# Unpacking 4-bit weights beside a matmul stream: integer codes on VectorE replaced by float arithmetic spread over VectorE and ScalarE

## The reference

```
xn = layernorm(x)
x  = x + gated_cumsum_attention(xn) + moe(xn)      # block 0: shared expert and 8 routed, top 2
xn = layernorm(x)
x  = x + latent_attention(xn) + ffn(xn)            # block 1
```

```
LUT = [0, .5, 1, 1.5, 2, 3, 4, 6, -0, -.5, -1, -1.5, -2, -3, -4, -6]
idx = stack([W & 15, W >> 4 & 15], -1)              # two codes a word
W_f32 = LUT[idx] * scale of its block of 32
```

## Time and profile before

| | us |
|---|---|
| median of 3 runs | 919.44 |
| lowest and highest | 918.81, 920.84 |
| the profiled execution | 919.44 |
| its span in the trace | 917.1 |
| TensorE matmul busy in the span | 796.1 (87%) |
| VectorE, ACT, GpSimd busy | 524.1 (57%), 435.9 (48%), 347.7 (38%) |

### The profile page before, as it was taken

How to read it: one execution, slowest core, us unless ns; L and a number is a source line. 1 busy time by engine, 2 the same in 40 slices (tenths; PEclk the granted TensorE clock), 3 DMA queues, 4 the chain that set the end, 5 groups by cost and what they waited for, 6 DMA issues and landing times.

```text
span 917.1 us, 12644 instructions
## 1 busy us (share of the span) xinstructions
PE 796.1 (87%) x4756; PEld 600.8 (66%) x4756; DVE 524.1 (57%) x871; ACT 435.9 (48%) x675; POOL 347.7 (38%) x277
## 2 busy tenths in 40 slices
PE   3759989998998899988898899798898897998886
PEld 1537866776676677766666677576676675776664
DVE  4742666675667633645464746564755656664735
ACT  3442433442434243352735754827645648536454
POOL 2333334662455242441342432424332515133533
PEclk9899999997999999998999999999999999999999
DMA  6331033332233125471110030110130200120100
GB/s 210 108 108 47 12 92 92 103 104 93 78 92 98 66 92 202 158 277 47 31 42 1 1 97 21 41 30 1 32 84 1 71 1 1 40 53 22 50 2 24
DMA packets 62171, 62.48 MB, mean 68 GB/s; under 512 B 6176, under 2 KB 52128, under 8 KB 61344
## 3 DMA queue, kind: packets, MB, share of 16 engines
q1 hardware_dynamic: 59680, 58.37, 20.6%
q10 hardware_dynamic: 2432, 3.32, 1.1%
HBM read 32.18 MB, written 16.78 MB: 53 GB/s over the span
## 4 chain that ended last, share of the span: by engine, by line
PE 53%; ACT 15%; DVE 13%; issue 10%; POOL 4%; DMA 4%; SPq 1%; ACTq 0%; DVEq 0%; POOLq 0%
PE ring L418 6%; PE ring L420 6%; PE ring L419 6%; PE acc L418 4%; PE acc L419 4%; PE acc L420 4%; ACT act L1027 3%; ACT L1027 2%; ACT ex L1027 2%; PE pm L418 2%; POOL hl L1128 2%; DVE hf L1392 2%; PE pm L420 2%; PE pm L419 2%; DMA x1s<-x 2%
## 5 line engine op out<-in xcount | busy, mean ns | idle before, releaser
L1128 POOL TENSOR_TENSOR hl<-hf,hh 128x512 fp32r<-128x512 f32 (+1 forms) x120 | 159.2, 1326 | 428.5 <-ACT hh L906 427.1
L418 PE MATMUL ring<-xh,wh 128*128 128x512 f32 (+1 forms) x272 | 114.0, 419 | 18.5 <-DVE xl L1226 13.4
L906 ACT ACTIVATE hh<-hf 128x512 fp32r<-128x512 f32 (+1 forms) x120 | 75.3, 627 | 92.1 <-DVE hf L1392 86.2
L418 PE MATMUL acc<-hh,wh 128*128 128x512 f32 (+1 forms) x240 | 101.2, 422 | 16.1 <-POOL hl L1128 16.1
L419 PE MATMUL ring<-xh,wl 128*128 128x512 f32 (+1 forms) x272 | 108.8, 400 | 0.0
L420 PE MATMUL ring<-xl,wh 128*128 128x512 f32 (+1 forms) x272 | 108.7, 400 | 0.0
L419 PE MATMUL acc<-hh,wl 128*128 128x512 f32 (+1 forms) x240 | 97.1, 405 | 0.0
L420 PE MATMUL acc<-hl,wh 128*128 128x512 f32 (+1 forms) x240 | 96.9, 404 | 0.0
L1286 DVE TENSOR_TENSOR hf<-act,ring 128x512 f32<-128x512 f32 (+1 forms) x56 | 38.3, 683 | 89.6 <-ACT act L896 86.6
L660 PE MATMUL ring<-qT,kT 98*128 98x256 bf16 (+1 forms) x256 | 45.6, 249 | 39.5 <-ACT ex L1027 20.3
L418 PEld LDWEIGHTS ring<-xh,wh 128*128 128x128 f32 (+1 forms) x272 | 52.0, 191 | 39.7 <-DVE xl L1226 16.3
(11 more groups left out here) (194 smaller groups left out, 1931.7 us busy)
## 6 DMA issues: line engine op xcount, KB each, us to landing
w4s<-w4h SPq DMA_DIRECT2D x24, 256.0 KB, 2.3
w4s<-w4l SPq DMA_DIRECT2D x24, 256.0 KB, 3.0
qT<-qp SPq DMA_DIRECT2D x96, 64.0 KB, 2.6
kT<-kp SPq DMA_DIRECT2D x96, 64.0 KB, 2.7
stage<-w SPq DMA_DIRECT2D x6, 704.0 KB, 5.5
wh<-w4s SPq DMA_DIRECT2D x2, 2048.0 KB, 9.4
wl<-w4s SPq DMA_DIRECT2D x2, 2048.0 KB, 14.3
words<-q SPq DMA_DIRECT2D x12, 256.0 KB, 3.3
```

Of the source, the lines that this page charges most:

```text
L418: pe.matmul(o, w_hi, x_hi, start=first, stop=False, skip_group_check=True)
L906: a.activation(h_parts(n)[0][0:rows, :], hf[0:rows, n % 2, :], ACT.Copy).then_inc(s_hh, 1)
L1128: return pool.tensor_tensor(dst, src, hi.bitcast(F32), ALU.subtract)
```

## The change

The float value of a code is now made by arithmetic. For each step VectorE shifts the three magnitude bits m to bit 22 of a 32-bit word and ORs a constant into the exponent (`fbits`), and puts the sign bit into `sbits`. ACT computes `gval = 8 * fbits - 1`. VectorE then takes `min(4 * fbits, gval)`, which is the value of the table, and ORs the sign in. GpSimd multiplies by the scale, which is used as it is, and has one buffer in place of two.

In VectorE's order the last two (value and sign of code k-1) stand at the beginning of step k, ahead of the three bit instructions for code k. ACT's `gval` of step k stands behind `w4h` in its step k and waits for the bits of step k.

```diff
-        mag = sb("mag", [P, QW], U16, c0)
-        sign = sb("sign", [P, QW], U16, c0)
-        code = sb("code", [P, 2, QW], U16, c0)
-        scl = sb("scl", [P, 2, QW], F32, c0)
+        fbits = sb("fbits", [P, QW], I32, c0)
+        sbits = sb("sbits", [P, QW], I32, c0)
+        gval = sb("gval", [P, 2, QW], F32, c0)
+        scl = sb("scl", [P, QW], F32, c0)
...
# SyncE
-                            sp.wait_ge(s_bits, 4 * (n - 1))
+                            sp.wait_ge(s_bits, 6 * (n - 1))
...
-                if k % 2 == 0:
-                    for n in (0, 1) if k == 0 else (k // 2 + 1,) if k // 2 + 1 < NQ else ():
-                        if n >= 2:
-                            sp.wait_ge(s_w, k)
-                        sp.dma_start(scl[:, n % 2, :], s4[:, n, :]).then_inc(s_scl[n % 2], 16)
+                if k % 2 == 0 and k < 2 * NQ:
+                    if k:
+                        sp.wait_ge(s_w, k)
+                    sp.dma_start(scl[:, :], s4[:, k // 2, :]).then_inc(s_scl, 16)
...
# ACT, behind w4h
-                if 0 <= k < 2 * NQ and k % 2 == 0:
-                    n = k // 2
-                    a.wait_ge(s_scl[n % 2], 16 * (n // 2 + 1))
-                    a.activation(scl[:, n % 2, :], scl[:, n % 2, :], ACT.Copy, scale=F4_UNIT).then_inc(s_sfit, 1)
+                if 0 <= k < 2 * NQ:
+                    a.wait_ge(s_bits, 3 * (k + 1))
+                    a.activation(gval[:, k % 2, :], fbits[:, :].bitcast(F32), ACT.Copy, bias=-1.0,
+                                 scale=8.0).then_inc(s_val, 1)
...
# GpSimd, behind w4l
-                    pool.wait_ge(s_code, k)
-                    pool.wait_ge(s_sfit, (k - 1) // 2 + 1)
+                    pool.wait_ge(s_sgn, 2 * k)
+                    pool.wait_ge(s_scl, 16 * ((k - 1) // 2 + 1))
...
-                    pool.tensor_tensor(wf[:, :], code[:, (k - 1) % 2, :].bitcast(F16), scl[:, (k - 1) // 2 % 2, :],
-                                       ALU.mult).then_inc(s_w, 1)
+                    pool.tensor_tensor(wf[:, :], gval[:, (k - 1) % 2, :], scl[:, :], ALU.mult).then_inc(s_w, 1)
...
# VectorE, dequant(k)
+                if 1 <= k < 2 * NQ + 1:
+                    v.wait_ge(s_val, k)
+                    val = gval[:, (k - 1) % 2, :]
+                    v.scalar_tensor_tensor(out=val, in0=fbits[:, :].bitcast(F32), scalar=4.0, in1=val, op0=ALU.mult,
+                                           op1=ALU.min).then_inc(s_sgn, 1)
+                    v.wait_ge(s_sgn, 2 * k - 1)
+                    v.tensor_tensor(val.bitcast(u32), val.bitcast(u32), sbits[:, :].bitcast(u32),
+                                    ALU.bitwise_or).then_inc(s_sgn, 1)
...
                     if k:
-                        v.wait_ge(s_code, k)
-                    low16 = words[:, k // 2 % 2, :].bitcast(U16).rearrange("p (n h) -> p n h", h=2)[:, :, 0]
-                    v.tensor_scalar(mag[:, :], low16, 9 - 4 * j, 7 << 9, ALU.logical_shift_left,
+                        v.wait_ge(s_sgn, 2 * k)
+                    w32, f32 = words[:, k // 2 % 2, :].bitcast(u32), fbits[:, :].bitcast(u32)
+                    v.tensor_scalar(f32, w32, 22 - 4 * j, 7 << 22, ALU.logical_shift_left,
                                     ALU.bitwise_and).then_inc(s_bits, 1)
-                    v.tensor_scalar(sign[:, :], low16, 12 - 4 * j, 1 << 15, ALU.logical_shift_left,
+                    v.tensor_scalar(sbits[:, :].bitcast(u32), w32, 28 - 4 * j, 1 << 31, ALU.logical_shift_left,
                                     ALU.bitwise_and).then_inc(s_bits, 1)
-                    v.wait_ge(s_bits, 2 * k + 2)
-                    if k >= 2:
-                        v.wait_ge(s_w, k - 1)
-                    v.tensor_tensor(code[:, j, :], mag[:, :], sign[:, :], ALU.bitwise_or).then_inc(s_code, 1)
+                    v.wait_ge(s_bits, 3 * k + 2)
+                    v.tensor_scalar(f32, f32, 124 << 23, None, ALU.bitwise_or).then_inc(s_bits, 1)
```

More of the change, by code:

```diff
@@ L77 @@
 Q0 = 8
-F4_UNIT = 2.0 ** 14
 W4_CUTS = [0, 4096, O_D4, O_D4 + 6 * D, O_D4 + T1 * D]
@@ L235, in transformer_blocks @@
         s_words = [sem(f'words_in{i}') for i in range(2)]
-        s_scl = [sem(f"scales_in{i}") for i in range(2)]
-        s_bits, s_sfit, s_code, s_w, s_w4h, s_w4l = map(
-            sem, ("bit_steps", "scales_fitted", "codes", "w4", "w4_hi", "w4_split"))
+        s_scl, s_bits, s_val, s_sgn, s_w, s_w4h, s_w4l = map(
+            sem, ("scales_in", "bit_steps", "values", "signs", "w4", "w4_hi", "w4_split"))
         s_w4out, s_w4in = [sem(f"w4_stored{i}") for i in range(2)], [sem(f"w4_in{i}") for i in range(4)]
@@ L1263, in turn_weights @@
                 v.tensor_tensor(own, own, part(0), ALU.add).then_inc(s_turnw, 1)
+            u32 = mybir.dt.uint32
             def dequant(k):
+                if 1 <= k < 2 * NQ + 1:
[6 more added lines that the diff above has]
+                                    ALU.bitwise_or).then_inc(s_sgn, 1)
                 if 0 <= k < 2 * NQ:
```

## The result

The changed kernel takes 961.23 us (median of four runs, 960.31 to 962.33); the kernel before takes 919.17 on the same chip (918.81 to 920.84). The ratio is 1.046, 95% interval 1.0445 to 1.0477: 42 us slower. The forecast was 955, with 930 to 976 as its range. The profiled execution took 962.32 us, its span 959.9 against 917.1 before.

The account below looks back on a forecast made before the run. TensorE was taken to set the pace, 4.43 us a tile, with VectorE and GpSimd excluding each other. Group growths of 5, 16, 12 and 2 us sum to +35, plus 1 for the clock: 919.4 + 36 = 955, range 930 to 976.

Parts of the forecast that it names:

- The odd tile: Second tile of each pair with unpacking steps: `act` to next `act` 7.45 us instead of 5.83.
- D1: VectorE's `scalar_tensor_tensor` making the value (4x against ACT's value), two float32 inputs: 0.69 us alone.
- D2: VectorE's OR of the sign into the value, two float32 inputs: 0.69 us alone.
- The crammed free and even tile: Tile without a step, then the next pair's first tile: together 9.1 us, a three-tile cycle of 16.55 against 13.3.
- fifth rival: Cycle right but pace milder, as GpSimd and VectorE do not meet everywhere: about 935; chance 0.12.
- The lock: Two-input VectorE instructions and GpSimd's exclude each other; without this the sum is near +15 us, with it +36.
- D3 to D5: VectorE's two shifts and OR on 32-bit words that make the bits: 0.42 us each alone, other end 0.69.
- third rival: The three 32-bit bit instructions take 0.69 us each: +19 less overlap, 971; chance 0.10.
- ACT's wait: `gval` waits for VectorE in 24 steps, 40 us or more; the `wf` wait shrinks below 58.5 or moves into it.
- The group ends: Time not given back where a group ends with a step: 3.35 us in the second group, 1.5 in the third.
- The four growths: Growth of the first block's four token groups: +5, +16, +12 and +2 us.
- fourth rival: Single scale buffer: scales land late for the odd step, 1 us in each of 12 places at worst; 960; chance 0.05.

Follow-up runs that it names:

- load_alone: Kernel before, with two more two-input float32 VectorE instructions at the head of each step, on spare data: 933.24 us, ratio 1.0134.
- change_ends: Changed kernel with the last tile's step put behind the next group's `xh` on ACT and `xl` on VectorE: 950.46 us, ratio 1.0331.
- before_w4h_late: Kernel before, with ACT's `w4h` alone one tile later, except in a group's last tile: 914.12 us, ratio 0.994.
- before_late_ends: before_w4h_late with the last tile's step behind the next group's `xh` on ACT and `xl` on VectorE: 908.06 us, ratio 0.9867.
- act_late_ends: act_late with the last tile's step behind the next group's `xh` on ACT and `xl` on VectorE: 920.47 us, ratio 1.0001.
- act_late: bits_first with ACT's `w4h` and `gval` one tile later, except in a group's last tile: 930.83 us, ratio 1.0107.
- bits_first: Changed kernel with float16 `gval`, 16-bit sign, and VectorE's bit instructions of code k ahead of value and sign of code k-1: 931.39 us, ratio 1.0132.

## Why the prediction was right

**The odd tile.** Predicted 7.45 us, measured 7.51. From `act` = 0, predicted and measured ends: D1 3.0 and 3.02, `w4l` 4.2 and 4.17, D2 4.75 and 4.72, `wf` 5.9 and 5.86, D5 6.9 and 6.94. The odd tiles of the second and third group that have no table load take 7.47 to 7.61.

**The crammed free and even tile.** Predicted 9.1, measured 9.27 (ACT's timeline of the changed kernel, third group):

```profile
272.73 0.58 ACT L893 ACTIVATE act<-ring 128x512 f32<-128x512 f32 x1
273.73 0.58 ACT L893 ACTIVATE act<-ring 128x512 f32<-128x512 f32 x1
...
281.46 0.63 ACT L886 ACTIVATE gval<-fbits 128x512 f32<-128x512 f32 x1 [2.94 <-DVE fbits L1285]
282.00 0.58 ACT L893 ACTIVATE act<-ring 128x512 f32<-128x512 f32 x1
```

A cycle of three tiles is 16.8 us, where I had 16.55 and TensorE needs 13.3. The other crammed pairs take 8.1 to 10.3. The first, uncrowded even tile of a group was to take 5.4; it takes 4.55 in the second group and 5.52 in the third. The fifth rival, a milder pace, did not come.

**The lock.** D1 has a median of 1.08 us and a least of 0.68, D2 1.66 and 0.69; what lies between is GpSimd. In the odd tile D1 ends 0.55 after `hl`, D2 0.55 after `w4l`, `fbits` 0.28 after `wf`. The Trainium skill ("SBUF — State Buffer", section "SBUF: two separate sides") was read as saying this for VectorE instructions with two SBUF inputs, and the trace agrees. No run here takes the lock away; load_alone shows only that such instructions have a price even where nobody waits for their result.

**D3 to D5.** Taken at 0.42, with 0.69 as the other end; they are 0.43 alone (`fbits` above), which rules the third rival out. By the tier table that the prediction cites from the Trainium skill ("VectorE: DVE Perf Modes") D3 to D5 were at 0.42, and the trace agrees, for uint32 words where the table's column is for float32.

**ACT's wait.** `gval` waits 47.6 us in 24 places, where I had 40 or more. One step failed in detail: ACT's wait for `wf` was to shrink below 58.5 or move into `gval`'s. It grew to 75.1. `w4h` stands ahead of `gval` in the queue and takes the first part of the wait: in the odd tile 4.80 are put down to `wf` and 0.45 to `fbits`, though it is `fbits` that sets the end. The forecast of the time did not hang on it: I had worked it out along ACT's queue, not from the list.

**The group ends: the term that was mis-sized.** The four growths are 2.2, 1.3, 1.8 and 2.5 us over what I had, all on one side. I gave the ends 3.35 and 1.5 us, from ACT's queue alone. That `xl` waits behind VectorE's step I had not counted. At the third group's end (timeline of the changed kernel):

```profile
336.69 0.63 ACT L886 ACTIVATE gval<-fbits 128x512 f32<-128x512 f32 x1 [3.19 <-DVE fbits L1285]
337.22 1.04 ACT L867 ACTIVATE xh<-xc 128x1024 fp32r<-128x1024 f32 x1
...
338.30 1.23 DVE L1222 TENSOR_TENSOR xl<-xc,xh 128x1024 fp32r<-128x1024 f32 x1 [1.64 <-ACT xh L867]
339.58 0.80 PE L415 MATMUL ring<-xh,wh 128*128 128x512 f32 x1 [3.36 <-DVE xl L1222]
```

The first matmul of the new group takes 0.80 us, where its like take about 0.42: it runs at the lower clock (stretches, columns as in the earlier trace rows).

```profile
339.00:343.00 4.00, 3.42 (x8) 2.75 (x9) 0.52 (x1) 0.46 (x1) 3.83 (x3) 0.50 0.05 16
```

change_ends puts the ends at 12 us in the changed kernel; before_w4h_late and before_late_ends put them at 7 in the kernel before (0.994 - 0.9867), so some 5 of the 42 come from here, by difference. TensorE's wait for `xl` says the same: 13.4 us before, 18.5 after, in each 10.1 of it at the kernel's start. Of the fourth group's +4.5, about 1.4 is this half clock: from its first `vs` to its second is 6.95 us (342.54 to 349.49) against 5.59 before. The 1 us that I had added for the clock was too little.

**The start.** Of the first group's +7.2, 1.6 us is there before any step runs: `act` of tile 8 is at 95.94 after and 94.33 before. Up to there the two kernels do the same work, and in the profiled executions of the other runs the very first `act` starts anywhere from 48.8 to 52.1 (51.75 after, 50.44 before). So this is most likely scatter and not the change.

**The scale buffer.** The fourth rival did not happen. GpSimd's idle time before `wf` is put down to its own `w4l` each time, as in the rows above, and the 12 loads land sooner than the 2.7 to 4.2 us of the earlier trace rows (view of the tile `scl`, after):

```profile
DMA to landing us min/median/max: 2.6/2.8/3.4
```

The prediction gave a load 5.4 us until the odd step's `wf`; measured, it is 5.5 (issued at 163.17, `wf` at 168.66). The 1.3 us that it then took off for `wf` were one too many, since 11.3 (7.45 + 3.85) is already where that `wf` begins.

**Where the 42 us are**, by what gives them back in the changed kernel: VectorE's order 22, the ends' order 12, the float32 width 8. Each was measured from another neighbour, so that their sum is 42 is partly luck, and of the ends' 12 the kernel before has 7 as well. The comparison of like with like is act_late_ends with before_late_ends: order and width repaired, and ACT and the ends arranged alike in both, the new arithmetic still costs 12.4 us. In the lists of waits TensorE then waits 5.0 us longer for VectorE's routed `hf` (6.7 against 1.7) and 2.3 longer for `xl` (14.9 against 12.6), which points at VectorE's longer step; no run shows what the 12.4 are made of. They aren't simply the 12 of load_alone, which lie mostly at an end whose order is repaired here. How much of the last 9.7 us, from act_late to act_late_ends, needs `w4h` and `gval` to be late as well was not tried either: bits_first with late ends alone was not run.

## What to carry to other kernels

When an in-order engine gets a new instruction that waits, write out what the releasing engine does first in the same tile, and do there first what somebody waits for; here the order of five instructions was worth 22 us. A wait and a load on the same loop can cost more than their sum: measure them together, since each alone showed a third of what the pair cost (12 and 11 of 36 us). Work that is due late must not stand ahead of the work that opens the next stage, even in a kernel that looks bound by TensorE: in the kernel before, moving it at the ends gave some 7 us, and `w4h` one tile later 5.5. And when a repair brings a changed kernel level with the old one, give the old one the same repair before calling the change free: here it gained 12 us by it.

## What the runs showed of the hardware

A 32-bit shift with mask on VectorE, 128x512, takes 0.43 us, as long as the 16-bit one that reads every second 16-bit element; a float32 `scalar_tensor_tensor` takes 0.68, as long as a plain product. In the odd tile above, an instruction on VectorE that was issued while GpSimd's ran ends 0.55 us after GpSimd's when it reads two float32 tensors, and 0.28 after it when it reads one. GpSimd pays too: `w4l`, 1.27 alone, takes 1.75 there, 0.48 longer, with 0.60 of D1 left when it starts. In the earlier trace rows it is 0.2 longer with 0.32 of `mag` left: not the whole rest, as the prediction reads it.

The clock was less regular than I had taken it. In load_alone three stretches with TensorE busy 1.5 of 4 us (304 to 316) were followed by a clock of 0.50 for 4 us of full work. In the kernel before, a stop of 2.51 us was followed by 0.74, and one of 2.47 us, at the third group's end (300.31), by 1.00 in the stretch from 300 to 304.
